# Graph network kernel: the second group's distance factors turned by VectorE and memory

## The reference, cut to what matters

```
h = relu(layernorm(x))
x_conv = relu(bn2(conv17(relu(bn1(conv1(h))))) + h)        # convolutions along the nodes
s = h @ w_se.T + b_se                                      # 3 numbers for each node
dist = sq[:, None] + sq[None, :] - 2 * s @ s.T             # sq = sum(s * s)
A = exp(-dist) * adj
x_nmp = A @ relu(h @ w_msg.T + b_msg)
r, z, n = gates of (x_conv, x_nmp) and h                   # a GRU cell
out = x + (1 - z) * n + z * h
```

## Time and profile before

| | |
|---|---|
| median of 3 runs | 281.51 us (281.49 to 281.79) |
| the profiled execution's own time | 281.62 us |
| its span, first to last instruction | 279.8 us |
| TensorE (PE) busy | 272.6 us, 97% |
| VectorE (DVE) busy | 244.4 us, 87% |
| ScalarE (ACT) busy | 163.9 us, 59% |
| GpSimd (POOL) busy | 64.7 us, 23% |
| granted TensorE clock, mean | 1.000 |
| DMA | 30.47 MB, mean 109 GB/s |

### The profile page before, as it was taken

One profiled execution on the slowest core, in us unless ns is written; L12 is line 12 of the kernel. 1 busy time (PEld: TensorE's weight loads), 2 busy tenths in 40 slices (PEclk: granted clock), 3 DMA queues, 4 the chain that ended last, 5 costly groups with the idle time before them and its releaser, 6 DMA issues.

```text
span 279.8 us, 5233 instructions
## 1 busy us (share of the span) xinstructions
PE 272.6 (97%) x1806; PEld 246.6 (88%) x1806; DVE 244.4 (87%) x550; ACT 163.9 (59%) x276; POOL 64.7 (23%) x126
## 2 busy tenths in 40 slices
PE   7999999999999999999999999999999999999993
PEld 6699977999889988899889998899888998899883
DVE  6999988998999889987999989988999887984666
ACT  3798458737654667526764467537674276541563
POOL 7800020930216002520206102430026100340000
PEclk9999999999999999999999999999999999999999
DMA  7910405665243554273642635464440604053002
GB/s 241 311 25 0 150 4 157 211 128 184 77 151 57 109 184 132 97 99 101 225 152 28 114 108 179 150 82 118 150 149 10 105 16 150 2 61 61 2 0 75
DMA packets 19741, 30.47 MB, mean 109 GB/s; under 512 B 9746, under 2 KB 13588, under 8 KB 18836
## 3 DMA queue, kind: packets, MB, share of 16 engines
q1 hardware_dynamic: 17024, 26.21, 28.6%
q0 software_dynamic: 2544, 3.93, 10.6%
q10 hardware_dynamic: 148, 0.01, 0.0%
HBM read 25.11 MB, written 8.70 MB: 121 GB/s over the span
## 4 chain that ended last, share of the span: by engine, by line
PE 90%; DVE 5%; ACT 2%; issue 1%; POOL 1%; DVEq 0%; ACTq 0%
PE ps L1327 24%; PE ps L1329 24%; PE ps L1328 23%; PE ps L1380 5%; PE ps L1423 4%; PE ps L1585 3%; PE ps L1446 2%; PE ps L1452 1%; PE ps L1455 1%; PE ps L1401 1%; ACT cp L554 1%; POOL rstd L417 1%; DVE stats L843 1%; DVE n_lo L1047 0%; PE ps L1376 0%
## 5 line engine op out<-in xcount | busy, mean ns | idle before, releaser
L1329 PE MATMUL ps<-v_hi,wt_lo 128*128 128x256 f32 x280 | 78.8, 281 | 0.0
L1327 PE MATMUL ps<-v_hi,wt_hi 128*128 128x256 f32 x280 | 78.7, 281 | 0.0
L1328 PE MATMUL ps<-v_lo,wt_hi 128*128 128x256 f32 x280 | 78.6, 281 | 0.0
L1327 PEld LDWEIGHTS ps<-v_hi,wt_hi 128*128 128x128 f32 x280 | 52.7, 188 | 0.6
L1328 PEld LDWEIGHTS ps<-v_lo,wt_hi 128*128 128x128 f32 x280 | 52.7, 188 | 0.6
L1329 PEld LDWEIGHTS ps<-v_hi,wt_lo 128*128 128x128 f32 x280 | 52.6, 188 | 0.0
L423 POOL TENSOR_TENSOR scale<-vpe,neg_half 128x8 f32<-128x8 f32 x6 | 10.6, 1768 | 84.6 <-DVE scale L860 84.6
L591 ACT ACTIVATE mbs<-ps,par 128x256 f32<-128x256 f32 x24 | 12.0, 501 | 29.7 <-DVE y L986 17.6
L1327 PE MATMUL ps<-h_hi,wt_hi 128*128 128x512 f32 (+1 forms) x67 | 26.7, 398 | 0.3 <-DVE h_lo L895 0.3
L1329 PE MATMUL ps<-h_hi,wt_lo 128*128 128x512 f32 (+1 forms) x67 | 25.8, 384 | 0.0
L1328 PE MATMUL ps<-h_lo,wt_hi 128*128 128x512 f32 (+1 forms) x67 | 25.7, 384 | 0.0
(11 more groups left out here) (171 smaller groups left out, 637.9 us busy)
## 6 DMA issues: line engine op xcount, KB each, us to landing
w<-ln_rows SPq DMA_DIRECT2D x6, 1024.0 KB, 4.6
mask<-adj_t SPq DMA_DIRECT2D x8, 512.0 KB, 3.6
out<-x_t SPq DMA_DIRECT2D x7, 512.0 KB, 5.1
out<-gate POOLq DMA_DIRECT2D x14, 256.0 KB, 4.2
xin<-x_nm SPq DMA_DIRECT2D x6, 512.0 KB, 4.2
xt<-x_t SPq DMA_DIRECT2D x6, 512.0 KB, 4.0
slot_rows<-turned SPq DMA_DIRECT2D x24, 32.0 KB, 3.0
rows<-slot_rows SPq DMA_DIRECT2D x6, 128.0 KB, 2.5
```

Of the source, the lines that this page charges most:

```text
L1327: pe.matmul(dst, wt_hi[:, blk, :], hi, start=start, stop=False)
L1328: pe.matmul(dst, wt_hi[:, blk, :], lo, start=False, stop=False)
L1329: return pe.matmul(dst, wt_lo[:, blk, :], hi, start=False, stop=stop)
```

## The change

`BY_TRANSPOSE` goes from 1 to 0, so the second group's slots are turned by VectorE and memory, and the second pass takes the later groups' order on TensorE, ScalarE and VectorE. Its slots are made by ScalarE and VectorE (`slots_first(1, ...)`, `slots_low_first(1, ...)`) and not by GpSimd. VectorE has a `turn(1)` ahead of the last `v_low_u(1, 2)`. The second pass's own differences in VectorE's order stay: both `join_b` and `add_h` ahead of `update(0, 1)`, `ln_apply(2, 1)` behind the first `join_y`. In the text, lines are those of the kernel before; in the changed one the same lines lie up to 3 lower or 6 higher.

```diff
--- before.py
+++ after.py
@@ -200,7 +200,7 @@
             sem("zd_ready"), sem("out_ready"))
 
 
-        BY_TRANSPOSE = 1
+        BY_TRANSPOSE = 0
 
         BY_MATMUL = 1
 
@@ -262,10 +262,7 @@
 
             engine.wait_ge(s_ready, 2 * g + 2)
 
-            if g <= BY_TRANSPOSE + 1:
-                upto(engine, rows_ps, g)
-            else:
-                engine.wait_ge(turned_ready, g - 1 - BY_TRANSPOSE)
+            engine.wait_ge(turned_ready, g - 1 - BY_TRANSPOSE)
             left, right = slots[:, 0], slots[:, 1]
 
             def twice(a):
@@ -275,7 +272,7 @@
                 return a[:, :, first:first + 6].rearrange("p b (r k) -> p b r k", k=3)
 
             s = s_sb[:, :, 0:3]
-            base = 10 * (g - 1)
+            base = 10 * (g - 2)
             engine.tensor_copy(six(left, 0), twice(s)).then_inc(s_steps, 1)
             engine.tensor_tensor(ssq[:], s, s, ALU.mult).then_inc(s_steps, 1)
             engine.wait_ge(s_steps, base + 2)
@@ -465,7 +462,8 @@
                 if g + 1 < NG:
                     ln_scale(g + 1)
                     pool.wait_ge(scale_ready, g)
-                distances(pool, g)
+                if g > 1:
+                    distances(pool, g)
 
                 pool.wait_ge(out_filled, 16 * g)
                 for c in range(NCH):
@@ -600,8 +598,8 @@
                 act.activation(s_sb[:, 0:6, :].rearrange("p (k b) d -> p k b d", b=3), both[:, 0:2, :, P:MW],
                                ACT.Copy).then_inc(s_ready, 1)
                 act.activation(s_sb[:, 6:8, :], both[:, 2, 0:2, P:MW], ACT.Copy).then_inc(s_ready, 1)
-                if g == 0:
-                    slots_first(0)
+                if g <= 1:
+                    slots_first(g, 0)
 
                 upto(act, nmp_ps, NCH * g)
                 act.activation(msg[:, 0:6, :].rearrange("p (k b) d -> p k b d", b=3), both[:, 0:2, :, 0:P],
@@ -614,25 +612,27 @@
                 act.activation(msg[:, 0:8, :], msg[:, 0:8, :], ACT.Relu).then_inc(msg_ready, 2)
 
 
-            def slots_first(step):
+            def slots_first(g, step):
                 left, right = slots[:, 0], slots[:, 1]
                 halves = right[:, :, 0:12].rearrange("p b (r h k) -> p b r h k", r=2, h=2)
                 hi = left[:, :, 0:6].rearrange("p b (r k) -> p b r k", k=3)
                 lo = left[:, :, 6:12].rearrange("p b (r k) -> p b r k", k=3)
                 if step == 0:
-                    act.wait_ge(s_ready, 2)
+                    act.wait_ge(s_ready, 2 * g + 2)
                     act.wait_ge(pool_set, 5)
+
+                    upto(act, rows_ps, g)
                     act.activation(hi, s_sb[:, :, 0:3].unsqueeze(2).broadcast_to([P, GB, 2, 3]),
                                    ACT.Copy).then_inc(slot_hi, 1)
                 elif step == 1:
-                    act.wait_ge(slot_hi, 1)
+                    act.wait_ge(slot_hi, 2 * g + 1)
                     act.activation(halves[:, :, :, 0, :], hi.bitcast(F32), ACT.Copy)
-                    act.wait_ge(slot_sq, 3)
+                    act.wait_ge(slot_sq, 3 * g + 3)
                     act.activation(left[:, :, 12], sq[:], ACT.Copy).then_inc(slot_hi, 1)
-                    act.wait_ge(slot_lo, 1)
+                    act.wait_ge(slot_lo, 2 * g + 1)
                     act.activation(halves[:, :, :, 1, :], lo.bitcast(F32), ACT.Copy)
                 else:
-                    act.wait_ge(slot_lo, 2)
+                    act.wait_ge(slot_lo, 2 * g + 2)
                     act.activation(right[:, :, 14:16], left[:, :, 12:14].bitcast(F32), ACT.Copy).then_inc(slots_ready, 1)
 
             def factor_rows(g):
@@ -743,9 +743,9 @@
                 lot_high(n)
             v_high_u(0, 1)
             messages(0, 3)
-            slots_first(1)
+            slots_first(0, 1)
             m_shared(0, 1)
-            slots_first(2)
+            slots_first(0, 2)
             lot_high(11)
             factor_rows(0)
             lot_high(12)
@@ -771,7 +771,9 @@
             v_high_b(1, 0)
             v_high_b(1, 1)
             messages(1)
+            slots_first(1, 1)
             v_high_u(1, 0)
+            slots_first(1, 2)
             v_high_u(1, 1)
             reset_rows(0, 1)
             for g in range(1, NG):
@@ -1064,24 +1066,24 @@
                 dve.transpose(turned[:].bitcast(F32).rearrange("p b (k s) -> p b k s", k=2),
                               slots[:, :, :, 0:KD].bitcast(F32).rearrange("p k b s -> p b k s")).then_inc(turned_ready, 1)
 
-            def slots_low_first(step):
+            def slots_low_first(g, step):
                 left = slots[:, 0]
                 s = s_sb[:, :, 0:3]
                 if step == 0:
-                    dve.wait_ge(s_ready, 2)
+                    dve.wait_ge(s_ready, 2 * g + 2)
                     dve.scalar_tensor_tensor(out=ssq[:], in0=s, scalar=-0.5, in1=s, op0=ALU.mult,
                                              op1=ALU.mult).then_inc(slot_sq, 1)
-                    dve.wait_ge(slot_hi, 1)
+                    dve.wait_ge(slot_hi, 2 * g + 1)
                     dve.tensor_tensor(left[:, :, 6:12].rearrange("p b (r k) -> p b r k", k=3),
                                       s.unsqueeze(2).broadcast_to([P, GB, 2, 3]),
                                       left[:, :, 0:6].rearrange("p b (r k) -> p b r k", k=3),
                                       ALU.subtract).then_inc(slot_lo, 1)
-                    dve.wait_ge(slot_sq, 1)
+                    dve.wait_ge(slot_sq, 3 * g + 1)
                     dve.tensor_tensor(sq[:], ssq[:, :, 0], ssq[:, :, 1], ALU.add).then_inc(slot_sq, 1)
-                    dve.wait_ge(slot_sq, 2)
+                    dve.wait_ge(slot_sq, 3 * g + 2)
                     dve.tensor_tensor(sq[:], sq[:], ssq[:, :, 2], ALU.add).then_inc(slot_sq, 1)
                     return
-                dve.wait_ge(slot_hi, 2)
+                dve.wait_ge(slot_hi, 2 * g + 2)
                 dve.tensor_tensor(left[:, :, 13], sq[:], left[:, :, 12], ALU.subtract).then_inc(slot_lo, 1)
 
             def update(g, c):
@@ -1186,9 +1188,9 @@
             lot_low(7)
             v_low_u(0, 1)
             join_b(0, 1)
-            slots_low_first(0)
+            slots_low_first(0, 0)
             v_low_u(0, 2)
-            slots_low_first(1)
+            slots_low_first(0, 1)
             lot_low(8)
             add_h(0)
             add_shared(0, 0)
@@ -1229,9 +1231,13 @@
             level1(1)
             v_low_b(1, 0)
             v_low_b(1, 1)
+            slots_low_first(1, 0)
             level2_u(1)
-            for part in range(3):
-                v_low_u(1, part)
+            slots_low_first(1, 1)
+            v_low_u(1, 0)
+            v_low_u(1, 1)
+            turn(1)
+            v_low_u(1, 2)
             reset(0, 1)
             for g in range(1, NG):
                 ahead = g + 1 < NG
```

## The result

The changed kernel takes 284.49 us (median of 6 runs, 283.42 to 285.79), the kernel before 281.65 (6 runs, 281.45 to 281.99): the ratio is 1.0102 with an interval of 1.0087 to 1.0116. It is slower, by 2.8 us (1%) where 2.0 were forecast, and it lies 0.2 us above the stated range. The profiled execution took 284.64 us, its span is 282.8. Its runs also differ by 2.4 us among themselves, where those of the kernel before differ by 0.5. In this document medians and ratios leave out four executions: one of hold_act at 448.41 us with a mean granted clock of 0.561, one of the kernel before beside it at 948.47, and two of order_free that lie over 1.5% above the fastest of their kernel (285.87 and 285.97).

The account below looks back on a forecast made before the run. TensorE, busy 97% of the span, was taken as the bound. Waits of 2.43 up to the gathers plus 0.08 after, less 0.55 saved, gave +1.96 us: 283.5 us, range 282.8 to 284.3.

Parts of the forecast that it names:

- its own saving: TensorE in the second group: fewer transposes and small distance matmuls, two wide ones added, saving 0.55 us if nothing waits.
- VectorE up to the eighth piece: Second group's convolution: the sum the eighth piece needs ends at 64.14, due 63.34, so TensorE waits 0.85 us.
- The exchange with ScalarE: Second group's slot making: ScalarE's high parts start at 53.7 instead of 52.94, and VectorE idles 0.13 us more.
- GpSimd's absence: VectorE without GpSimd's slot work beside it: gains 0.2 us at most, taken as 0.
- The chain to the gathers: Second group's ScalarE and VectorE up to the first mask's product: gathers start at 71.15, due 68.72, TensorE losing 2.43 us.
- The turned slots' way through memory.: Second group's slots, stored and reloaded, land at about 65.2, up to 1.4 later behind the column load; no cost until 67.1.
- GpSimd's 11 instructions: Slot work taken off GpSimd: costed at 0, as nobody on the path waited for it except the slots.
- The second rival: Second group's slots land late beside the 1 MB load and an earlier output add: 0.6 to 2.0 us more, chance 0.10.
- The clock: Granted clock assumed at full level in every stretch, as in the kernel before.
- rivals 2 and 3: Slots landing late: 0.6 to 2.0 more, chance 0.10; more path shifts at gates or convolution sums: 0.3 to 0.8, chance 0.07.
- a chain shorter by 0.7: Allowance for the second group's ScalarE and VectorE path to the gathers, setting the range's low end of 282.8 us.

Follow-up runs that it names:

- hold_act: hold_add with ScalarE's shared part of the last convolution row and exponentials ahead of its two copies by graphs in the second group: 282.08 us, ratio 1.0021.
- order_free: all_order without the held second add: 284.40 us, ratio 1.0079.
- hold_add: Changed kernel with GpSimd's second add of the first group's output held until the second group's factor rows have landed: 283.62 us, ratio 1.0066.
- hold_both: Changed kernel, in its own order, with both adds of the first group's output held until the factor rows have landed: 283.40 us, ratio 1.0061.
- xt_early: Changed kernel with the load of x for the fourth group ahead of the factor stores, no add held: 283.52 us, ratio 1.0066.
- all_order: hold_add with earlier turn, next rows' halves, last sums and masks moved, ScalarE's shared part and exponentials earlier in the second group: 282.23 us, ratio 1.0023.
- ctl_after: Changed kernel run again without any edit: 284.46 us, ratio 1.0093.
- all_quiet: all_order with both adds of the first group's output held, not only the second: 281.34 us, ratio 0.9991 against the kernel before.
- quiet_x: all_quiet with the load of x for the fourth group moved behind the load of the mask: 281.41 us, ratio 0.9992 against the kernel before.

## Why the prediction was wrong

- **The direction and the place were right.** The loss is in the second group alone, TensorE waits there and nowhere later, and the loss is what it waits less its own saving: 3.70 - 0.55 = 3.15 us.
- **VectorE up to the eighth piece**: forecast 0.85 us later than due, measured 0.70 (0.53 of it is idle time in the profile's count). The exchange with ScalarE was as drawn, each station some 0.1 to 0.2 earlier. VectorE's stretch without what was added took what it took before: GpSimd's absence gave VectorE at most 0.1, where the prediction allowed 0.2 and took 0. In the trace of the kernel before it is GpSimd's own time that differs: its copy of 128x48 takes 0.65 us at 54.39, beside a VectorE subtraction with both inputs in SBUF, and 0.23 at 55.58, beside one that reads PSUM. Why, is not shown; that VectorE subtraction takes 0.69 to 0.72 us over the whole run.
- **The chain to the gathers**: forecast 71.15 and 283.5 us, measured 71.01 and 283.62 with the slots in time (hold_add; 283.40 in hold_both), and 1.5 us less once ScalarE's order was mended (hold_act). This term held, within 0.2 us at each station.
- **The step that failed is "The turned slots' way through memory."** It gave 65.2 for the landing, allowed 1.4 for the column load and called the cost nothing up to 67.1. The limit was right (xt_early lands at 67.0 and pays 0.13), the landing was 68.2. In the profiled execution all of that is the last load: it was issued at 62.70, where the forecast's chain has it too (65.2 - 2.5), and took 5.5 us and not 2.5. The 2.5 was taken from later groups: in the third to fifth a load of x stands behind the last load as well, but the second add is issued 4.2 to 4.9 us ahead of it; here it is 1.0. With the second add held the last load takes 2.3 us (hold_add), and with both held the chain lands by 64.5 (hold_both). The second part is the first add. The sum costed GpSimd's 11 instructions at 0, "which nobody on the path waited for", and did not follow what the freed GpSimd does next: it issues an add of 256 KB 5.9 us earlier, ahead of the column load, and the stores behind that load end 0.6 to 1.9 us later than with the add held. The second rival names this earlier add and gave lateness of the slots 0.10; its price of 0.6 to 2.0 more is what came (the median is 1.0 above the forecast). It does not name the second add, which did not move and did more: in the order of all_order, holding it took 2.2 us off the median, holding the first too 0.9 more.
- **The clock** was assumed at full level. Late slots alone put the gathers at 72.36 where hold_add has them at 71.01, 1.35 us, and the profile of ctl_after loses another 1.5 to the clock. Runs from 283.4 to 286.2 are what these two parts, each present or not, would give: near hold_add's time without either, 284.0 to 284.6 with late slots, 285.7 to 286.2 with the lower clock as well, which the mean clocks of the runs bear out. How late the slots were is seen in the two profiled runs only.
- **The range** of 282.8 to 284.3 covered the forecast's own terms and none of this. It claimed to take in "most of rivals 2 and 3", though rival 2's own price began at 284.1 and ran to 285.5, above the range's end of 284.3. Its low end, a chain shorter by 0.7, no run in the changed kernel's own order shows: there the gathers started at 71.01 in hold_add and 70.82 in hold_both, 0.14 and 0.33 before the forecast's 71.15.

## What to carry to other kernels

When a change puts a chain of small transfers on the path, draw every large transfer beside it at its time, those that stay as well as those that move; and when work is taken off an engine that also issues transfers, expect its transfers to move earlier (the first add by 5.9 us here) before costing the removal at nothing. A wait on small dependent transfers should be measured next to the large ones that will be its neighbours, not at a quiet place of the same program (the last load took 2.5 us as the median over the kernel before, 5.5 beside the second add). Moving a stage to another order asks for the whole order: the path gave a gain, 0.3 us of its 0.55, only after ScalarE's copies, the masks and the adds had moved too.

## What the runs showed of the hardware

- A 128 KB load landed 5.5 us (the changed kernel), 4.6 (ctl_after) and 4.1 (order_free) after its issue with an add of 256 KB from GpSimd's queue issued 1.0, 1.6 and 1.4 us ahead of it and a load of 512 KB behind it. With the add 2.1 us ahead and no such load it took 3.2 (xt_early), with the load and no second add 2.3 to 3.1 (hold_add, hold_act, all_order, all_quiet, hold_both), with neither 2.4 (quiet_x).
- A 1 MB load took 6.7 to 8.0 us with an add of 256 KB issued 1.3 us ahead of it and 4.3 to 4.6 with that add held. Four 32 KB stores issued behind it took 4.5 to 5.9 us in the first case and 4.0 in the second.
- In the kernel before, a GpSimd copy of 128x48 took 0.65 us (at 54.39) beside a VectorE instruction with both inputs in SBUF and 0.23 (at 55.58) beside one with an input in PSUM.
- TensorE's granted clock was 0.50 from 68.75 to 72.00 us behind an idle time of 2.28 us in one execution (ctl_after) and stayed at 1.00 behind one of 2.62 us in another of the same kernel. Behind the waits of 1.3, 1.0 and 2.1 us in xt_early, hold_act and order_free it stayed at 1.00 too. So of the two executions of the changed kernel the one with the longer wait kept the clock and the one with the shorter lost it; what decides it is not shown.
